# Multiplying zeros on TensorE around the last norm and the first head, and two pairs of score banks instead of three

## The reference, cut to what matters

```
x = x + 0.5 * moe(layernorm(x))          # 8 experts, top 2, hidden 256, silu-gated
x = x + attention(layernorm(x))          # 16 heads of 8, rotary on q and k, bias on q, k, v and out
x = x + 0.5 * moe(layernorm(x))          # the same expert weights again
```

## Time and profile before

| | us |
|---|---|
| median of 3 runs (lowest, highest) | 1265.86 (1265.64, 1267.74) |
| the profiled execution, its own time | 1268.65 |
| its span, first to last instruction | 1266.9 |
| TensorE busy | 1235.2 (98%) |
| VectorE busy | 1113.5 (88%) |
| ScalarE busy | 799.7 (63%) |
| GpSimd busy | 143.8 (11%) |
| TensorE's mean granted clock | 0.983 |

### The profile page before, as it was taken

How to read it: one execution, slowest core, us unless ns; L and a number is a source line. 1 busy time by engine, 2 the same in 40 slices (tenths; PEclk the granted TensorE clock), 3 DMA queues, 4 the chain that set the end, 5 groups by cost and what they waited for, 6 DMA issues and landing times.

```text
span 1266.9 us, 32082 instructions
## 1 busy us (share of the span) xinstructions
PE 1235.2 (98%) x10208; PEld 610.7 (48%) x10208; DVE 1113.5 (88%) x2262; ACT 799.7 (63%) x1540; POOL 143.8 (11%) x450
## 2 busy tenths in 40 slices
PE   6999999999899999999999999999999999999998
PEld 4766667667522222222222222222225777767776
DVE  7889878898889999999999999999985777777775
ACT  5433333333239999999999999999995333323332
POOL 0021122201231111111111111111110000000000
PEclk9999999999959999999999999999999999999999
DMA  7000111012111111111111111111111000000000
GB/s 212 1 30 24 49 51 38 26 39 69 50 57 36 42 32 42 32 42 32 42 32 35 39 32 42 32 42 32 42 41 47 11 27 20 28 28 26 9 9 9
DMA packets 54201, 48.36 MB, mean 38 GB/s; under 512 B 11632, under 2 KB 46960, under 8 KB 54128
## 3 DMA queue, kind: packets, MB, share of 16 engines
q1 hardware_dynamic: 54128, 47.48, 12.2%
HBM read 23.73 MB, written 23.33 MB: 37 GB/s over the span
## 4 chain that ended last, share of the span: by engine, by line
PE 92%; DVE 5%; issue 1%; ACT 1%; DMA 0%; DVEq 0%; ACTq 0%
PE ps L826 25%; PE ps L981 23%; PE ps L966 22%; PE ps L813 17%; PE ps L784 1%; PE ps L803 1%; PE ps L751 1%; PE ps L933 1%; DVE mx L1228 1%; DVE X L1174 1%; PE ps L820 1%; DVE act L1162 1%; ACT probs L725 0%; PE ps L790 0%; DVE tmp L1072 0%
## 5 line engine op out<-in xcount | busy, mean ns | idle before, releaser
L1228 DVE TENSOR_REDUCE mx<-ps 128x1 f32<-128x1024 f32 x512 | 586.0, 1216 | 6.4 <-PE ps L933 2.5
L725 ACT ACTIVATE probs<-ps 128x512 f32<-128x512 f32 x1024 | 551.4, 600 | 32.2 <-PE ps L966 27.9
L654 ACT ACTIVATE sg<-ps,unscale 128x512 f32<-128x512 f32 x256 | 173.8, 687 | 281.9 <-PE ps L826 265.6
L981 PE MATMUL ps<-probs,vh 128*32 128x256 f32 x4096 | 328.2, 392 | 0.0
L966 PE MATMUL ps<-Q,K 51*128 51x512 bf16 x1024 | 321.4, 384 | 1.8 <-ACT probs L725 0.4
L933 PE MATMUL ps<-K,Q 48*128 48x512 bf16 x1008 | 319.2, 388 | 3.1 <-DVE mx L1228 2.5
L813 PEld LDWEIGHTS ps<-w,act 128*128 128x128 f32 x2048 | 248.7, 192 | 18.3 <-issue 1.4
L813 PE MATMUL ps<-w,act 128*128 128x128 f32 x2048 | 249.8, 275 | 0.0
L1162 DVE SCALAR_TENSOR_TENSOR act<-ps,unscale,sg 128x512 f32<-128x512 f32 x256 | 183.1, 745 | 56.8 <-ACT sg L654 18.1
L826 PE MATMUL ps<-x_hi,w_hi 128*128 128x512 f16 x512 | 196.0, 383 | 6.9 <-DVE act L1162 5.6
L826 PE MATMUL ps<-x_hi,w_lo 128*128 128x512 f16 x512 | 196.1, 383 | 0.0
(11 more groups left out here) (84 smaller groups left out, 597.8 us busy)
## 6 DMA issues: line engine op xcount, KB each, us to landing
o_parts<-ot SPq DMA_DIRECT2D x64, 128.0 KB, 1.9
q_stack<-parts SPq DMA_DIRECT2D x96, 64.0 KB, 2.0
k_stack<-parts SPq DMA_DIRECT2D x96, 64.0 KB, 2.0
Q<-q_stack SPq DMA_DIRECT2D x64, 96.0 KB, 2.3
K<-k_stack SPq DMA_DIRECT2D x64, 96.0 KB, 2.3
probs<-w_in SPq DMA_DIRECT2D x8, 256.0 KB, 4.9
att<-o_parts SPq DMA_DIRECT2D x16, 128.0 KB, 2.6
rden<-rdens SPq DMA_DIRECT2D x16, 128.0 KB, 2.5
```

Of the source, the lines that this page charges most:

```text
L654: nc.scalar.activation(sg[:, j, :], hid[2 * j], ACT.Silu, scale=unscale[:, e, 2 + j:3 + j]).then_inc(silu_done, 1)
L725: nc.scalar.activation(probs[:, kb % PSLOTS, j * CH:(j + 1) * CH], score[u][i], ACT.Exp, scale=SCALE).then_inc(probs_ready, 1)
L981: last = nc.tensor.matmul(opsum[u][VW * c:VW * (c + 1), :], vh[:, u % 2, kb, :], probs[:, kb % PSLOTS, c * QW:(c + 1) * QW], start=(kb == ...
L1228: nc.vector.tensor_reduce(mx[:, u % 2, t:t + 1], pair.rearrange("p a b -> p (a b)"), AX_X, ALU.max).then_inc(max_read, 1)
```

## The change

A tile `blank` of 128 × 512 bf16 zeros is set by GpSimd at the program's start. A helper `blanks(count, bank)` multiplies its first 128 columns with all of it, into a PSUM bank that nobody reads then. It is called 20 times between the wait for the last `acc_done` and the transposes of the last norm; twice after each of tiles 4 to 7 of the first head's maxima; twice after `values`; and twice after each pair of matmuls of head 1's maxima.

`FIRST_PAIRS` becomes 2, so that the first head's maxima use banks 0 to 3 alone. The wait for `acc_done` moves from tile 2 to tile 4. Tiles 2 and 3 are issued ahead of it, `x2_transposes` comes before tile 4, both `q_or_k` before tile 5, and VectorE's two `rotate` come before tiles 5 and 7 (before: 4 and 7).

```diff
@@ constants @@
-FIRST_PAIRS = 3
+FIRST_PAIRS = 2
+BLANKS = 20
+FEW_BLANKS = 2
@@ build @@
+        blank = sb("blank", [P, CH], BF16)
...
+        idle_bank = ps[:, 4, :]
+        free_score = ps[:, [s for s in SCORE_BANKS if s != BANKS.row[0]][0], :]
@@ gpsimd @@
             seq = Order(pool, pool_order)
 
+            seq.mark(nc.gpsimd.memset(blank[:], 0.0))
             seq.then(nc.gpsimd.memset(ident[:], 0.0))
@@ tensor, first_max_scores @@
                     pe.wait_ge(head_loaded[0], 32)
-                elif t == 2:
-                    pe.wait_ge(acc_done, E * NCH)
                 at_least(pe, max_read, t - FIRST_PAIRS + 1)
@@ tensor, after ffn(0, False) @@
+            def blanks(count, bank):
+                for _ in range(count):
+                    nc.tensor.matmul(bank, blank[:, 0:P], blank[:], start=True, stop=True)
+
             for t in range(2, KB):
-                if t == FIRST_PAIRS:
+                if t == 4:
+                    pe.wait_ge(acc_done, E * NCH)
+                    blanks(BLANKS, idle_bank)
                     x2_transposes(NCH - 1)
-                if t == FIRST_PAIRS + 1:
+                if t == 5:
                     q_or_k(NCH - 1, 0)
-                if t == 2 * FIRST_PAIRS + 1:
                     q_or_k(NCH - 1, 1)
                 first_max_scores(t)
+                if t >= 4:
+                    blanks(FEW_BLANKS, idle_bank)
             values(NCH - 1)
+            blanks(FEW_BLANKS, idle_bank)
@@ tensor, maxima of head 1 @@
                 max_scores(0, 1, i)
+                if i % 2:
+                    blanks(FEW_BLANKS, free_score)
@@ vector, after norm2 @@
             for t in range(2, KB):
-                if t == FIRST_PAIRS + 1:
+                if t == 5:
                     rotate(last_chunk, 1, 0)
-                if t == 2 * FIRST_PAIRS + 1:
+                if t == 7:
                     rotate(last_chunk, 1, 1)
                 first_max(t)
```

## The result

The change made the kernel slower: 1269.98 us (median of 9 executions, 1268.51 to 1273.2) against 1266.29 (9, 1265.63 to 1270.23), a ratio of 1.0024 with a 95% interval of 1.0013 to 1.0035. The prediction was 1263.4, with a range up to 1268.2, so the time lies above it and the sign is the other one. The profiled execution took 1269.78 us, its span is 1268.0.

A forecast was written before the change was run, and what follows sets the result against it. VectorE was taken to set the pace from the last norm into the heads, with TensorE at half clock for 34.1 us. Terms 0 + 0 + 2.6 − 0.1 = 2.5 us off 1265.86 gave 1263.4 us, range 1261.3 to 1268.2.

The forecast's parts named there:

- The blank tile at the start: Program start: the tile's memset on GpSimd takes 0.4 us and ends before x lands; costs nothing, at most 0.1 us.
- Twenty blanks: Before the last norm's transposes: 4.3 us of zeros, hidden by VectorE's norm chain with 0.9 us to spare; clock stays up.
- Two pairs of banks: First head's maxima: VectorE's 1.04 us wait goes, and the first rotary step starts 0.75 us earlier.
- SyncE is late next: First head's last half tile, i = 15, waits for head 3's load on SyncE's queue; gain 2.6 us, not 5.5.
- The clock at i = 15: First head's last half tile: a clock fall in its 2.9 us wait costs up to 1.7 us.
- the fall before head 1: Gap of 2.4 us before head 1: a 3.41 us clock fall costs 1.1 us, swallowed by the wait at i = 15.
- Rival 2: Head 1: clock falls and stays down, blanks become the bound; 1268.7 (chance 0.12), or 1272.5 if zeros hold nothing (0.06).
- The rule that I weighed: Gap before head 1: sustained activity releases the throttle, so a fall there ends soon and the sum stays 1263.4.
- Rival 3: SyncE's queue before i = 15 does not bind, as stores or landings are quicker; gain 5.1 to 5.5 us, 1260.6, chance 0.08.
- That zeros might not hold the clock: Last norm: clock falls at 343.36 as before despite the zeros, key scores start at 374.9; 1272.5, chance 0.06.

The follow-up runs named there:

- the last version: Changed kernel with 12 zeros for 2 behind the values, head 3 loaded early, wait for all stores moved behind head 1's maxima rows: 1263.5 us, ratio 0.9964.

## Why the prediction was wrong, point by point

- **The blank tile at the start: right.** Its memset took 0.53 us (0.4 assumed), and GpSimd's last constant ended at 3.55, before x landed.
- **Twenty blanks: right.** They kept the clock at 1.00 across the norm in every profile that has them, ended 0.68 us before the transposes and cost nothing.
- **Two pairs of banks: right.** The first rotary step started 8.5 us behind the last addition (348.35), against 9.3 before; 0.86 us earlier instead of 0.75.
- **SyncE is late next: right in kind, 0.8 off in size.** i = 15 waited 3.31 us for head 3. Head 3's k part took 3.2 us from issue to release (374.07 to 377.29) where the earlier trace rows gave a median of 2.3 and a maximum of 2.9; the same load took 2.3 in the profile of before. Why it took longer here no row shows. So i = 15 gained 1.8 us, not 2.6.
- **The clock at i = 15: the term was too small.** I allowed 1.7 us at most for a fall there. In the profiled execution it lasted 6.82 us and turned a lead of 1.8 us into a lag of 1.0, that is 2.8 us. The fall in the earlier trace rows had lasted 3.4, and I took its length for the length of a fall.
- **The failed step** is the one on the fall before head 1: "costs 3.41 × (1 − 1.165/1.71) = 1.1 us, and the 2.9 us wait at i = 15 swallows it". The gap was forecast (2.4 us; 2.24 measured), so was the price of a pair with its zeros at half clock (1.71; 1.93 measured). What was wrong was the length: in the two further profiles of the changed kernel the fall lasted 20.5 and 23.9 us and took in about six of the eight pairs, so key scores started 30.7 and 31.2 us behind the last addition, against 25.9 without the zeros between the pairs. The wait at i = 15 was too short to swallow 5 us: i = 15 came at 41.7 and 43.2, where the sum has 36.6 (377.1 less 340.5) and the kernel before 39.2. Rival 2 said exactly this and put it at 1268.7 with a chance of 0.12 for this form, though the earlier trace rows had already shown TensorE busy 11.70 of 11.70 us at 0.50 with no return. The row should have had more of the say than the one fall of 3.4 us.
- **The rule that I weighed.** From 358.49 to 371.42 TensorE is shown busy 12.93 of 12.93 us at 0.50, half of it matmuls of 48 rows. The Trainium skill, page "TensorE: Matmul & The Clock Gate", section "What's actually happening", has sustained activity release the throttle; the trace does not bear it out for these matmuls.
- **Rival 3's number** (5.1 to 5.5 us if SyncE did not bind) is what the last version reached, 5.3, once both waits on that queue and the gap were gone. I had put it down to quicker transfers; it needed another order on the queue. In time only the two executions without a fall, 1260.80 and 1261.01, came to its 1260.6; the median is 1263.5.
- **That zeros might not hold the clock** is refuted: the clock stayed at 1.00 through 4.3 us of nothing else and, with the few zeros, on to the gap before head 1.

## What to carry to other kernels

Filler work on an engine is priced at the clock that it is meant to prevent. If it leaves one gap in which the clock can fall, then the filler behind that gap runs at half speed and becomes the bound; fill the widest gap first, and between units that another engine paces put filler only where it fits at half clock too, or where every gap ahead is closed. When a stage gets faster, read every in-order queue that feeds the next one for what now lands last, DMA queues above all. And when a profiled execution's mean clock differs from that of most executions, take another profile before explaining the median with it.

## What the runs showed of the hardware that was not expected

Falls of the clock lasted very different times: 3.4 us among 128-row f16 matmuls in the expert layer (182.93 to 186.34), 3.4 or 6.8 us at the start of the heads, 6.8 us in the last head, and 17 to 24 us from head 1 on, among 48-row matmuls alone or mixed half and half with 128-row zeros. With the zeros TensorE was shown busy nearly all of that time (23.82 of 23.89 us, 20.41 of 20.48). What sets the length is not shown: only one edit changed what follows a gap and nothing else, the zeros between the pairs taken out, and in its one profile the fall lasted 17.1 us against 20.5 and 23.9.

The same instructions did not always lose the clock: behind the gap of 2.23 us before head 1 it held in one profile of the changed kernel and fell in the two others, at 358.69 and 358.49. What decides that, no row shows. It stays open also why the fall in the last head, which costs 2.6 to 3.1 us, is in two of three profiles of the changed kernel and in those of three versions, and not in that of before. No single wait of TensorE ahead of it is over 0.5 us. All five profiles with it are of kernels with zeros between the pairs of head 1, some 600 us earlier; three more profiles of such kernels do not have it, and none of the five without these zeros. No run was made on it, and a part of the difference between medians may be due to it.
